# A fused adaLN attention and mixture layer on one core: K/V tiles of a batch together, residual folded into x ahead

## The reference

```
h = layernorm(x) * (1 + ca) + sa
Xn = layernorm(h) * gamma + beta
Q, K, V = Xn @ W_in + b_in
K, V = rotary(K), rotary(V)                  # on half of the features
A = 0.5 * sum_over_rows(cos(K) * cos(V)) + 0.5   # one number for each feature
x = x + ga * ((A * Q) @ W_out + b_out + h)
h2 = layernorm(x) * (1 + cb) + sb
x = x + gb * (relu(h2 @ W_up.T) @ W_down.T + s * (h2 @ W_expert))   # s: sum of the top 2 routing weights
```

## Time and profile before

| | us |
|---|---|
| median of three runs | 385.25 |
| the profiled execution | 386.43 |
| its span, first to last instruction | 384.6 |
| PE busy | 367.0 |
| DVE busy | 255.4 |
| ACT busy | 166.7 |
| POOL busy | 113.3 |

### The profile page before, as it was taken

One profiled execution on the slowest core, in us unless ns is written; L12 is line 12 of the kernel. 1 busy time (PEld: TensorE's weight loads), 2 busy tenths in 40 slices (PEclk: granted clock), 3 DMA queues, 4 the chain that ended last, 5 costly groups with the idle time before them and its releaser, 6 DMA issues.

```text
span 384.6 us, 4649 instructions
## 1 busy us (share of the span) xinstructions
PE 367.0 (95%) x1664; PEld 286.9 (75%) x1664; DVE 255.4 (66%) x515; ACT 166.7 (43%) x293; POOL 113.3 (29%) x110
## 2 busy tenths in 40 slices
PE   4997999899997999989999999999999999999996
PEld 0155888678885888868788878888788878887885
DVE  0677799869978488876887559727550855084354
ACT  1337388884427821075314681247114612541210
POOL 0114683276932528425163151910000001000000
PEclk9988899999999899999999999999999999999999
DMA  7995964050030000000000002100200110011002
GB/s 222 378 388 191 348 258 168 0 164 2 2 82 2 0 0 2 27 2 2 0 27 2 0 0 111 28 2 27 82 2 0 55 56 0 0 57 55 2 0 109
DMA packets 10951, 27.42 MB, mean 71 GB/s; under 512 B 1185, under 2 KB 1569, under 8 KB 9777
## 3 DMA queue, kind: packets, MB, share of 16 engines
q1 hardware_dynamic: 10928, 27.13, 19.8%
HBM read 22.90 MB, written 4.23 MB: 71 GB/s over the span
## 4 chain that ended last, share of the span: by engine, by line
PE 66%; DVE 12%; issue 7%; ACT 6%; DMA 4%; POOL 2%; SPq 1%; DVEq 0%; ACTq 0%; POOLq 0%
PE ps L1032 19%; PE ps L1034 19%; PE ps L1033 19%; PE ps L1039 3%; PE ps L1056 2%; DMA xs<-in_wmod 2%; DMA xs<-in_X 2%; ACT sqj L444 2%; DVE hb L657 1%; PE ps L1047 1%; ACT ps L493 1%; DVE ps L690 1%; PE ps L1159 1%; PE ps L1160 1%; ACT t_hi L495 1%
## 5 line engine op out<-in xcount | busy, mean ns | idle before, releaser
L1032 PE MATMUL ps<-w_hi,t_hi 128*128 128x512 f32 x192 | 75.7, 394 | 0.0
L1034 PE MATMUL ps<-w_hi,t_lo 128*128 128x512 f32 x192 | 75.2, 392 | 0.0
L1033 PE MATMUL ps<-w_lo,t_hi 128*128 128x512 f32 x192 | 75.2, 392 | 0.0
L1032 PE MATMUL ps<-t_hi,w_hi 128*128 128x512 f32 x128 | 51.6, 403 | 0.0
L1032 PE MATMUL ps<-w_hi,g_hi 128*128 128x512 f32 (+1 forms) x132 | 51.3, 389 | 0.3 <-DVE g_lo L743 0.3
L1034 PE MATMUL ps<-w_hi,g_lo 128*128 128x512 f32 (+1 forms) x132 | 50.6, 383 | 0.0
L1033 PE MATMUL ps<-w_lo,g_hi 128*128 128x512 f32 (+1 forms) x132 | 50.5, 383 | 0.0
L1034 PE MATMUL ps<-t_hi,w_lo 128*128 128x512 f32 x128 | 50.4, 393 | 0.0
L1033 PE MATMUL ps<-t_lo,w_hi 128*128 128x512 f32 x128 | 50.4, 393 | 0.0
L683 DVE TENSOR_TENSOR t_lo<-ps,t_hi 128x512 fp32r<-128x512 f32 x32 | 21.8, 688 | 32.9 <-ACT t_hi L495 32.6
L1032 PEld LDWEIGHTS ps<-w_hi,t_hi 128*128 128x128 f32 x192 | 36.5, 190 | 7.6
(11 more groups left out here) (130 smaller groups left out, 613.8 us busy)
## 6 DMA issues: line engine op xcount, KB each, us to landing
xs<-in_X SPq DMA_DIRECT2D x4, 1024.0 KB, 7.5
stage<-in_w SPq DMA_DIRECT2D x4, 1024.0 KB, 6.8
out<-xs SPq DMA_DIRECT2D x15, 256.0 KB, 2.0
xs<-in_wmod SPq DMA_DIRECT2D x3, 1024.0 KB, 9.8
xs<-in_wmod SPq DMA_DIRECT2D x8, 256.0 KB, 7.0
stage<-in_w SPq DMA_DIRECT2D x8, 256.0 KB, 9.6
gate_bc<-mod_rows SPq DMA_DIRECT2D x8, 256.0 KB, 6.7
gate_bc<-in_wmod SPq DMA_DIRECT2D x1, 1024.0 KB, 11.9
```

What stands on the lines that cost most here:

```text
L1032: mm(dst, l_hi, r_hi, start=start, stop=False)
L1033: mm(dst, l_hi, r_lo, start=False, stop=False)
L1034: return mm(dst, l_lo, r_hi, start=False, stop=stop)
```

## The change

It does five things.

1. PE takes the four K/V tiles of a batch together, tiles 0 and 2 in X_PAIR and 1 and 3 in Y_PAIR. Then come the output projection of the batch before, `a_sums` of this batch (in batch 0 it stays behind Q), and Q with the transposes.
2. Q's banks are 2, 3, 4, 5. The output rows are in banks 4, 5, 0, 1 (the last batch: 4, 5, 2, 3). The waits for free banks follow.
3. From batch 1 on A is known when Q is multiplied, so Q's chunks are evicted one by one behind Q in the same batch on ACT and split on DVE, between the transposes' evictions and splits. Batch 0's Q is still evicted after its sums.
4. `base` and POOL's `x2_out` go. POOL computes ahead x = x + ga * (h + b_out), three instructions a row tile (`residual`); DVE's `x2_out` then multiplies PSUM by the gate into free rows of hb and adds to x, for all four tiles, 32 instructions in all as before.
5. The order of the rest is new: h's rows and statistics come at other places among the tiles, `normalise` takes four rows at once, W_up's and W_expert's splits come ahead of the last batch's Q. POOL's additions of batch 0 no longer wait for `split_lo_out`: residual(0, 0) stands before weight(0, 3), the other three after `rstd_x(2)`.

The core of the diff, by engine:

```diff
-Q_BANKS = (4, 5, 2, 3)
-O_BANKS = (4, 5, 2, 3)
+Q_BANKS = (2, 3, 4, 5)
+O_BANKS = ((4, 5, 0, 1), (4, 5, 0, 1), (4, 5, 0, 1), (4, 5, 2, 3))
...
-        def kv_pair(b, t):
-            return Y_PAIR if t == 2 or (b == 0 and t == 0) else X_PAIR
+        def kv_pair(t):
+            return Y_PAIR if t % 2 else X_PAIR
...
             def load_gate_b(b):
-                sp.wait_ge(x2_dve, b * 2 + 2)
-                sp.wait_ge(x2_pool, b * 2 + 2)
+                sp.wait_ge(x2_s, b * NT + NT)
```

POOL, with its order in batch 0:

```diff
+            def residual(g, t):
+                n = g * NT + t
+                h, x = h_row_of(g, t), xs[:, tok(g, t)]
+                pool.wait_ge(z_s, n + 1)
                 nc.gpsimd.tensor_tensor(h, h, bo_bc[:], ALU.add).then_inc(base_s, 1)
+                pool.wait_ge(base_s, n * 3 + 1)
+                nc.gpsimd.tensor_tensor(h, h, gate_bc[:, g * D:(g + 1) * D], ALU.mult).then_inc(base_s, 1)
+                pool.wait_ge(base_s, n * 3 + 2)
+                nc.gpsimd.tensor_tensor(x, x, h, ALU.add).then_inc(base_s, 1)
...
+            def attention_first():
+                rstd_x(1)
+                weight(0, 0)
+                for t in range(3):
+                    scale_rows(1, t)
+                weight(0, 1)
+                scale_rows(1, 3)
+                rstd_h(1, 0, 2)
+                weight(0, 2)
+                rstd_h(1, 2, 2)
+                pool.wait_ge(const_in, N_CONST)
+                pool.wait_ge(ga_in, B * 16)
+                residual(0, 0)
+                weight(0, 3)
+                rstd_x(2)
+                for t in range(1, NT):
+                    residual(0, t)
```

ACT in batches 1 to 3:

```diff
+            def attention(b):
+                norm_sums(b, 0)
+                if b + 2 < B:
+                    x_sums(b + 2)
+                norm_sums(b, 1)
+                if b + 2 < B:
+                    x_squares(b + 2)
+                normalise(b + 1, 0, NT)
+                norm_sums(b, 2)
+                norm_sums(b, 3)
+                if b == B - 1:
+                    split_hi(5)
+                    split_hi(4)
+                q_evac(b, 0)
+                q_evac(b, 1)
+                t_evac(b + 1, 0)
+                t_evac(b + 1, 1)
+                q_evac(b, 2)
+                t_evac(b + 1, 2)
+                t_evac(b + 1, 3)
+                q_evac(b, 3)
```

DVE:

```diff
+            def x2_out(b, t):
+                n = b * NT + t
+                y = hb[:, (b + 1) % 2, t, :]
+                dve.wait_ge(o_ps, n + 1)
+                dve.wait_ge(base_s, ((b + 1) * NT + t + 1) * 3 if b < B - 1 else B * NT * 3)
+                v.tensor_tensor(y, ps[:, O_BANKS[b][t], :], gate_bc[:, b * D:(b + 1) * D], ALU.mult).then_inc(o_y, 1)
+                dve.wait_ge(o_y, n + 1)
+                v.tensor_tensor(xs[:, tok(b, t)], xs[:, tok(b, t)], y, ALU.add).then_inc(x2_s, 1)
```

DVE's order in batches 1 to 3 (lines without a sign stood there before):

```diff
             def attention(b):
+                more = b < B - 1
+                if b == 1:
                     for c in range(NC):
+                        q_split(0, c)
+                if more:
                     h_row(b + 1, 0)
                     h_row(b + 1, 1)
+                kv_rows(b, 0)
+                kv_products(b, 0)
+                if more:
+                    h_row(b + 1, 2)
+                    h_row(b + 1, 3)
+                kv_sum(b, 0)
+                if more:
                     h_stats(b + 1, 0)
                     h_stats(b + 1, 1)
+                else:
+                    x2_rows(B, 0)
+                    x2_rows(B, 1)
+                kv_rows(b, 1)
+                if b + 2 < B:
+                    x_mean(b + 2)
+                kv_products(b, 1)
+                if more:
                     h_stats(b + 1, 2)
                     h_stats(b + 1, 3)
                 else:
+                    x2_rows(B, 2)
+                    x2_rows(B, 3)
+                h_aggr(b + 1, 0, NT)
                 kv_sum(b, 1)
+                h_shift(b + 1, 0, NT)
                 kv_rows(b, 2)
                 kv_products(b, 2)
                 kv_sum(b, 2)
+                if b + 2 < B:
+                    x_var(b + 2)
                 kv_rows(b, 3)
                 kv_products(b, 3)
+                x2_out(b - 1, 0)
+                kv_sum(b, 3)
+                a_pairs(b)
+                x2_out(b - 1, 1)
+                if b + 2 < B:
+                    x_shift(b + 2)
+                x2_out(b - 1, 2)
+                a_evac(b)
+                x2_out(b - 1, 3)
+                if not more:
+                    split_lo(4)
+                q_split(b, 0)
+                q_split(b, 1)
                 t_split(b + 1, 0)
                 t_split(b + 1, 1)
+                q_split(b, 2)
                 t_split(b + 1, 2)
                 t_split(b + 1, 3)
+                q_split(b, 3)
```

PE:

```diff
             def kv_tile(b, t):
+                n = b * NT + t
+                if t >= 2:
+                    pe.wait_ge(kv_sb, n - 1)
+                    pe.wait_ge(kprod, n - 1)
+                elif t == 1:
+                    wait(pe, q_los, (b - 1) * NC + 2)
+                elif b == 1:
+                    pe.wait_ge(kv_sb, 3)
+                    pe.wait_ge(kprod, 3)
+                else:
+                    wait(pe, o_y, (b - 1) * NT)
...
             def attention(b):
-                kv_tile(b, 0)
+                for t in range(NT):
+                    kv_tile(b, t)
                 if b > 0:
                     out_rows_of(b - 1)
-                for t in range(1, NT):
-                    kv_tile(b, t)
+                    a_sums(b)
                 for c in range(NC):
                     if c < 2:
-                        wait(pe, o_y, (b - 1) * NT + c + 1)
+                        pe.wait_ge(kv_sb, b * NT + 4)
+                        pe.wait_ge(kprod, b * NT + 4)
                     else:
-                        pe.wait_ge(kv_sb, b * NT + 3)
-                        pe.wait_ge(kprod, b * NT + 3)
+                        wait(pe, o_y, (b - 1) * NT + c - 1)
                     feature_chunk(b, Q_BANKS[c], WQ, c, q_ps)
...
-                a_sums(b)
+                if b == 0:
+                    a_sums(0)
```

More of the change, by code:

```diff
@@ L400, in attention @@
-                pool.wait_ge(afold, b * 3 + 3)
-                if b == 0:
-                    pool.wait_ge(const_in, N_CONST)
-                    pool.wait_ge(wlo_out, NC)
-                    for t in range(NT):
-                        base(0, t)
-                if b < B - 1:
-                    for t in range(NT):
-                        base(b + 1, t)
+                if b == 1:
+                    residual(1, 0)
+                weight(b, 1)
+                if more:
+                    rstd_h(b + 1, 0, NT)
+                else:
+                    rstd_h(B, 0, NT)
@@ new lines, in attention @@
+                if b == 1:
+                    residual(1, 1)
+                weight(b, 2)
+                if b == 1:
+                    residual(1, 2)
+                elif more:
+                    residual(b + 1, 0)
+                weight(b, 3)
+                if b + 2 < B:
+                    rstd_x(b + 2)
+                if b == 1:
+                    residual(1, 3)
+                    residual(2, 0)
+                if more:
+                    for t in range(1, NT):
+                        residual(b + 1, t)
@@ L417, in _ @@
             low_part(2, whi, (1,) * NC, wlo_q)
-            for b in range(B):
+            attention_first()
+            for b in range(1, B):
                 attention(b)
             rstd_h(B + 1, 0, NT)
-            x2_out(B - 1, 2)
-            x2_out(B - 1, 3)
             low_part(6, whi, (5,) * NC, wlo_down)
@@ L591, in ffn @@
                     e_evac(b, 3)
-            split_hi(4)
-            for c in range(NC):
-                q_evac(B - 1, c)
             split_hi(6)
@@ new lines, in q_splits_from, with attention_first @@
+            def q_splits_from(b, c0):
+                for c in range(c0, NC):
+                    q_split(b, c)
+            def attention_first():
+                x_stats(1)
+                x_aggr(1)
+                dve.wait_ge(const_in, N_CONST)
+                dve.wait_ge(row_out, 32)
+                kv_rows(0, 0)
+                x_shift(1)
+                kv_products(0, 0)
+                kv_sum(0, 0)
+                kv_rows(0, 1)
+                kv_products(0, 1)
+                h_row(1, 0)
+                h_row(1, 1)
+                h_stats(1, 0)
+                h_stats(1, 1)
+                h_aggr(1, 0, 2)
+                x_mean(2)
+                kv_sum(0, 1)
+                kv_rows(0, 2)
+                h_shift(1, 0, 2)
+                h_row(1, 2)
+                h_row(1, 3)
+                h_stats(1, 2)
+                h_stats(1, 3)
+                h_aggr(1, 2, 2)
+                kv_products(0, 2)
+                h_shift(1, 2, 2)
+                kv_sum(0, 2)
+                kv_rows(0, 3)
+                kv_products(0, 3)
+                t_split(1, 0)
```

(27 more changed lines are left out.)

204 lines of the change are left out of this document (42 added, 162 removed).

## The result

| | before | after |
|---|---|---|
| median, us | 385.66 (4 runs, 383.77 to 386.62) | 430.41 (4 runs, 429.23 to 431.96) |
| profiled execution, us | 386.43 | 431.4 |
| its span | 384.6 | 429.5 |
| mean granted clock | 0.982 | 0.936 |

The ratio is 1.1169, with an interval of 1.1107 to 1.1232. The change costs 44.8 us where I had forecast 27.7. The time is 7.4 us above the upper end of the range.

The account below looks back on a forecast made before the run. PE, a queue of matmuls, was taken as the bound, so only its waits count. Terms of +10.3 up to batch 1's K/V, then +14.4, +1.4 and +1.6 for batches 1 to 3 gave +27.7 us: 413.0 us, range 394 to 423.

Parts of the forecast that it names:

- one loss and a half: Slow-clock matmuls after PE's stands: 1.5 us behind batch 0's stand, 0.8 behind batch 1's sums.
- DVE keeps up: Batch 3: without h_row and with one-operand x2_rows, DVE is in time for the sums; batch 48.2 us, +1.6.
- 2.6 late: Batch 2: two or three collisions with POOL delay the sums by 2.6 us; batch 49.5 us, +1.4.
- Batch 1's chain without a collision: DVE's work from L613 to a_pairs(1), including waits but no POOL collisions: 37.1 us.
- So PE stands from 62.0 to at least 70.7: Batch 0: Q's new banks make PE wait until DVE has read K/V tile 3, 8.7 us.
- P: Start of batch 0's Q on PE: 70.7 plus 2.2 us for two collisions, 72.9.
- T1: Start of batch 1's K/V on PE: forecast 88.1, 10.3 us later than before.
- 13 collisions, 14.3 us: Batch 1, up to the pairs: DVE instructions lengthened by POOL's streams, taken between bounds of 0 and 22.
- T2: Start of batch 2's K/V on PE: forecast 154.0, against 129.25 before.
- half a clock loss, 0.8: Batch 1, behind the sums: 0.8 us for matmuls slowed by a lower clock.
- Rival 3: DVE bounds batch 2 too and is hit each time, 22 collisions in batch 1, 6 in batch 2: 425.5 us, chance 0.15.
- Rivals 1 and 2: First: DVE reads tile 3 in time, not slower, chance 0.07. Second: batch 0's stand alone, no collisions, 393 us, 0.20.

Follow-up runs that it names:

- e4: The changed kernel with 28, 24 and 12 more matmuls, results unused, before the sums of batches 1, 2 and 3: 426.03 us.
- e8: The changed kernel, but POOL's low part of W_expert in batch 3 waits for DVE's pairs again, as before the change: 424.59 us.
- e1: The changed kernel, but batch 0's Q uses banks 4, 5, 2, 3 again and K/V tile (1, 1) waits for all four splits: 425.94 us.
- e3: The changed kernel without POOL's 48 residual instructions, so h + b_out times the gate is missing from x: 408.42 us.

## Why the prediction was right in its direction and wrong in its size

The mechanism held: PE stands on DVE's chain, and POOL's streams lengthen that chain. What failed are four terms of the sum, all too small. The clock was priced at one loss and a half; 7.7 of the 17.6 us missed lie behind the sums, and e4 gives 7.4 of them back. Batch 3's "DVE keeps up" missed 3.3, which e8 puts on `low_part(5)`. Batch 2's "2.6 late" missed 3.5. Batch 1's chain without a collision, 37.1 us, was the fourth; it missed 3.1 net.

**Batch 0, right.** "So PE stands from 62.0 to at least 70.7" and two collisions of 1.1 gave P = 72.9; Q started at 72.72 after 10.46 us. Exactly two instructions, L706 and L675, took 1.40 and 1.21 us beside residual(0, 0). The clock behind the stand cost 1.7 us where 1.5 was priced. T1 was 88.02 for 88.1. e1 adds what the choice of banks is worth: somewhat over half of the stand, as the rest comes back at the transposes and Q's third chunk. The price of 1.1 us a collision was right by a lucky choice: the L718 of the earlier trace rows is a tensor_scalar on 128x768 and I held it against L613 on 128x512, but undisturbed it takes 0.61, the same.

**Batch 1, POOL without its wait, right in mechanism.** L611 took 5.79 us instead of 2.49 and L736 1.03 us. The stand before tile 1 was 4.90 us for my 6.7, those before tiles 2 and 3 were 1.77 and 2.77 for "about 3 each", and that before the sums 6.95 for 5 to 6.

**Batch 1, the chain to the sums: collisions nearly right, the rest short.** For 13 collisions, 14.3 us, the residual alone made 13, worth 13.0 us of the stretch (e3). But my 13 were to hold those of scale_rows too, and these come on top: in e3 the first two h_rows still took 3.43 us instead of 1.28. So there were 15, and that the count came near is partly luck, for they lie elsewhere: four, not six, from L613 to ab_col; three on the h_rows, as taken; and eight on the running sums, the fold, L675 and L633, where I had taken four. The term of 37.1 us without any was short: without residual the sums come 41 us after T1, not 36.6. Of these 4.4 us, 1.90 are DVE's wait for scale_rows, for which I had nothing, and 2.15 the two h_rows; the rest I can't place. The net miss is 3.1 us.

**Batch 2, wrong: "two or three collisions make it 2.6 late".** The stand before the sums was 5.97. e3, with 34.4 us instead of 38.8, gives the residual beside DVE 4.4 us, where I had 2.6. The rest is scale_rows: in the trace after, POOL does it from 161.78 to 167.72 and DVE reaches tile 0's rows only at T2 + 7.1. I had written that "tile 0 is not ready before T2 + 5.5" and taken the lateness as hidden; 1.6 of it was not. Its cause was not the 15 residual instructions either: POOL was through with them and idle for 4.23 us, waiting for ACT's z. The two h_rows beside scale_rows then took 1.77 us each for 0.69. This was not tried by itself.

**Batch 3, wrong: "DVE keeps up".** By DVE's own work it did, as e8 shows. It failed to price low_part(5), which the diff frees of its wait and which cost 3.3 us before the sums: the same kind of edit that I had priced in batch 0 (a POOL stream let go ahead of a DVE chain), not looked for in batch 3.

**The clock, wrong: "half a clock loss, 0.8".** I priced one loss behind the first stand and a half behind the sums of batch 1, and wrote of none in batches 2 and 3, although my own sum had a stand of 2.6 us in batch 2. The rows from 98.62 on show the behaviour: behind a stand of 4.90 us matmuls start 0.43 us apart (99.21 is followed by 99.64) instead of 0.23, and the granted clock over these 4 us is 0.50, the 1.2 GHz level (columns as in the windows above):

```profile
98.00:102.00 4.00, 3.38 (x8) 2.74 (x9) 1.95 (x3) 2.32 (x4) 3.32 (x3) 0.50 0.54 150
```

Counted from such starts, the stands of 10.46, 4.90, 2.77, 6.95, 5.97 and 3.16 us were followed by 1.7, 2.3, 1.7, 2.0, 2.8 and 1.7 us lost, the one of 1.77 us by 0.1; and the eight small matmuls of the sums took 1.7 us instead of 0.8 in batches 1 and 2. Behind the sums this makes up most of the missed 2.4, 4.0 and 1.3 us of my table. e4 shows it: with the stands filled, 7.4 us of the same stretches are gone.

**The rivals.** Rival 3 (DVE bound in batch 2 as well, 425.5) was nearest, with 22 collisions in batch 1 for a measured 15; it came near by adding too much in batch 1 and leaving out the clock. Its sign, batch 2 over 53 us, was met: 57.0. Rivals 1 and 2 are out: batches 1 to 3 took 71.4, 57.0 and 52.8.

**The rule of ports.** Where POOL streams, most of DVE's instructions on two SBUF operands took 0.9 to 1.1 us longer, whatever their size; the last addition of x2_out (L751, 128x512) took 0.4 to 0.6 longer, and one that started just ahead of POOL's next took its own time. L699, with one operand in PSUM, took 680 to 683 ns all 16 times. The rule cited in the prediction (the Trainium skill, SBUF — State Buffer, "Who interferes with whom") is that a VectorE instruction with two SBUF inputs contends with a GpSimd instruction that reads SBUF. The trace agrees, for scalar_tensor_tensor (L718, 2.02 for 1.01) as well. Two SBUF operands are not the whole of it, though: two instructions with a single tensor operand, both tensor_scalar, were hit alike (L715 1.65 us for 0.61, L633 1.24 for 0.16), while bn_stats (L659) beside the same stream kept its 0.68. POOL pays too: its residual instructions took up to 2.00 us for 1.27, and its busy time grew by 29.1 us where 16 more at 1.27 make 20.3.

## What to carry to other kernels

When every tile of a stage is put before its reduction, the engine that folds the tiles gets a deadline, and what GpSimd streams through SBUF beside it counts against that deadline. So list each wait that a diff drops from GpSimd's order and price what then runs beside VectorE. Give every longer TensorE stand a clock term of its own, and ask of a stand early in a chain which other wait is late behind it: of the 10.5 us seen here, new banks gave back 4.5 by the medians.
